# Neighbourhood attention of layer 0: ScalarE's copies and exponentials in turn, products with V ahead of the transposes, eight images written out

## The reference

```python
q = (x @ Wq + bq).reshape(B, nh, H, W, lr) * scale     # B 4, nh 8, H = W = 56, lr 4
k = (x @ Wk + bk).reshape(B, nh, H, W, lr)
v = (x @ Wv + bv).reshape(B, nh, H, W, hd)             # hd 32
k_win = k[:, :, idx_h][:, :, :, :, idx_w]              # the 7 x 7 keys around each token
v_win = v[:, :, idx_h][:, :, :, :, idx_w]
attn = jnp.einsum('bhijc,bhikjlc->bhijkl', q, k_win) + bias
attn = jax.nn.softmax(attn.reshape(B, nh, H, W, 49), axis=-1).reshape(B, nh, H, W, 7, 7)
out = jnp.einsum('bhijkl,bhikjld->bhijd', attn, v_win)
```

## Time and profile before

| what | value |
|---|---|
| median of 3 runs | 8468.63 us (8464.75 to 8475.0) |
| the profiled execution, its own time | 8475.56 us |
| its span, first to last instruction | 8473.8 us |
| `layer0_attend`, first score matmul to last store issued | 494.49 to 1606.54, 1112.05 us |
| TensorE busy share of the whole span | 86% |
| mean granted TensorE clock, whole span | 0.871 |
| mean granted TensorE clock, this stage | 0.59 |

### The profile page before, as it was taken

One profiled execution on the slowest core, in us unless ns is written; L12 is line 12 of the kernel. 1 busy time (PEld: TensorE's weight loads), 2 busy tenths in 40 slices (PEclk: granted clock), 3 DMA queues, 4 the chain that ended last, 5 costly groups with the idle time before them and its releaser, 6 DMA issues. The chain is left out here.

```text
span 8473.8 us, 153009 instructions
## 1 busy us (share of the span) xinstructions
PE 7312.5 (86%) x45616; PEld 4411.8 (52%) x45616; DVE 5407.8 (64%) x12877; ACT 4098.8 (48%) x9367; POOL 3701.9 (44%) x2395
## 2 busy tenths in 40 slices
PE   4457787898999999999999999999999888087877
PEld 3345565565545545455455455554553336076766
DVE  3357777666977767677677677776773017166666
ACT  0057777521025655556566566565656651033332
POOL 4010000111026666666666666566666663543432
PEclk8756555798579999999999999999999998598888
DMA  5432221487001120211210212112111016111110
GB/s 156 136 94 62 60 66 48 116 253 202 0 16 34 30 61 23 65 25 36 54 37 25 62 28 48 44 36 54 30 29 42 4 45 210 31 38 45 43 44 23
DMA packets 403203, 520.46 MB, mean 61 GB/s; under 512 B 64096, under 2 KB 355474, under 8 KB 399063
## 3 DMA queue, kind: packets, MB, share of 16 engines
q1 hardware_dynamic: 379687, 469.02, 20.6%
q0 software_dynamic: 22640, 40.75, 1.7%
HBM read 339.07 MB, written 200.10 MB: 64 GB/s over the span
## 5 line engine op out<-in xcount | busy, mean ns | idle before, releaser
L1253 DVE TENSOR_REDUCE a_tops<-a_ps 128x1 f32<-128x448 f32 (+1 forms) x5600 | 3070.8, 613 | 1085.6 <-PE a_ps L1155 1068.2
L1376 POOL TENSOR_TENSOR a_added<-a_P 128x896 f32<-128x896 f32 x1344 | 2800.3, 2104 | 2087.5 <-ACT a_P L1353 2087.5
L1353 ACT ACTIVATE a_P<-a_ps 128x448 f32<-128x448 f32 (+1 forms) x5600 | 2656.6, 547 | 2114.8 <-PE a_ps L1224 2083.0
L1224 PE MATMUL a_ps<-a_qp,a_kp 98*128 98x448 f32 (+1 forms) x5600 | 2155.6, 400 | 97.5 <-ACT a_P L1353 72.9
L1155 PE MATMUL a_ps<-a_hk,a_hq 96*128 96x448 f32 (+1 forms) x4900 | 1818.2, 381 | 1.9 <-DMA a_hq<-scratch_q 1.9
L1224 PEld LDWEIGHTS a_ps<-a_qp,a_kp 98*128 98x128 f32 (+1 forms) x5600 | 1029.7, 187 | 1289.5 <-ACT a_P L1353 736.3
L1175 PE MATMUL a_ps<-a_P,a_vt 128*32 128x448 f32 (+1 forms) x11200 | 1334.3, 548 | 0.0
L1155 PEld LDWEIGHTS a_ps<-a_hk,a_hq 96*128 96x128 f32 (+1 forms) x4900 | 916.6, 187 | 262.8 <-DVE a_tops L1253 170.9
L462 PE MATMUL n_ps<-n_idn,n_P 112*98 112x112 f32 x2688 | 523.6, 368 | 187.1 <-DVE n_P L519 168.0
L1191 PE MATMUL a_ps<-a_added,a_ones 128*32 128x448 f32 x5376 | 649.0, 555 | 0.0
L462 PEld LDWEIGHTS n_ps<-n_idn,n_P 112*98 112x98 f32 x2688 | 410.3, 181 | 288.2 <-DVE n_P L519 266.3
(11 more groups left out here) (193 smaller groups left out, 7674.9 us busy)
## 6 DMA issues: line engine op xcount, KB each, us to landing
a_qp<-scratch_q SPq DMA_DIRECT2D x168, 224.0 KB, 3.9
a_kp<-scratch_k SPq DMA_DIRECT2D x96, 320.0 KB, 5.5
a_hk<-scratch_k SPq DMA_DIRECT2D x84, 336.0 KB, 5.0
scratch_t<-o_ts SPq DMA_DIRECT2D x56, 448.0 KB, 5.6
scratch_vw<-scratch_v SPq DMA_DIRECT2D x56, 392.0 KB
n_vt<-scratch_vw SPq DMA_DIRECT2D x64, 343.0 KB
a_hq<-scratch_q SPq DMA_DIRECT2D x84, 200.0 KB, 3.2
e_w<-in_w SPq DMA_DIRECT2D x16, 1024.0 KB
```

Of the source, the lines that this page charges most:

```text
L1224: pe.matmul(PS[0:rows_of(t), i_s % 3, 0:GW], kp[0:98, hh, 128 * t:128 * t + rows_of(t)], qp[0:98, hh, GW * j:GW * j + GW], start=True, sto ...
L1253: dve.tensor_reduce(tops[0:rows_of(t), KT * hh + t, k:k + 1], PS[0:rows_of(t), bank, 0:GW], AX_X, ALU.max).then_inc(topped, 1)
L1353: act.activation(P[0:rows_of(t), (2 * n + pair) % (2 * RING), hh % 2, :], PS[0:rows_of(t), (4 * n + hh) % 3, 0:GW], ACT.Exp).then_inc(expe ...
L1376: pool.tensor_tensor(added2[:, a % 6, :, :], P[:, (2 * n + pair) % (2 * RING), :, :], P[:, (2 * n + 2 + pair) % (2 * RING), :, :], ALU.add ...
```

## The change

Four things change, all in `layer0_attend`. The computation and the number of matmuls, activations, VectorE instructions and DMAs stay as they are.

1. ScalarE takes the copies of the block before and the exponentials of this block in turn: C(n-1) head 0, E(n) head 0, C(n-1) head 1, E(n) head 1, and so on. The last four copies follow at the end of the stage.
2. TensorE does S(n), M(n-2), T(n-1), where it did S(n), T(n-1), M(n-2).
3. All eight images are written out on TensorE, ScalarE, VectorE, GpSimd and SyncE; the loops are gone, and waits compare with constants.
4. The increments of `steps` are gone with them.

```diff
             def body(it, first):
                 for n in range(NBLK):
                     scores(it, n)
+                    if n >= 2:
+                        mix(it, n - 2)
+                    elif not first:
+                        mix(it - 1, NBLK - 2 + n)
                     if n >= 1:
                         turn(it, n - 1)
                     elif not first:
                         turn(it - 1, NBLK - 1)
-                    if n >= 2:
-                        mix(it, n - 2)
-                    elif not first:
-                        mix(it - 1, NBLK - 2 + n)
 
             pe.wait_ge(consts, 16)
             pe.wait_ge(zeroed, 3)
-            body(0, True)
-            with pe.Fori(1, ITS) as it:
-                body(it, False)
+            for it in range(ITS):
+                body(it, it == 0)
+            mix(ITS - 1, NBLK - 2)
             turn(ITS - 1, NBLK - 1)
-            mix(ITS - 1, NBLK - 2)
             mix(ITS - 1, NBLK - 1)
...
-            def body(it):
+            def body(it, first):
                 for n in range(NBLK):
-                    exponentials(it, n)
-                    copy_turned(it, n)
-
-            body(0)
-            with act.Fori(1, ITS) as it:
-                body(it)
+                    for hh in range(4):
+                        if n >= 1:
+                            copy_turned(it, 4 * n - 4 + hh)
+                        elif not first:
+                            copy_turned(it - 1, U - 4 + hh)
+                        exponential(it, 4 * n + hh)
+
+            for it in range(ITS):
+                body(it, it == 0)
+            for hh in range(4):
+                copy_turned(ITS - 1, U - 4 + hh)
```

More of the change, by code:

```diff
@@ L325, in layer0_attend @@
         mixed, out_read, stored = sem("mixed"), sem("out_read"), sem("stored")
-        steps = sem("steps")
         def since(eng, semaphore, it, each, k):
-            if not isinstance(it, int) or it * each + k > 0:
+            if it * each + k > 0:
                 eng.wait_ge(semaphore, it * each + k)
@@ L369, in store, with body @@
                 sp.wait_ge(out_read, it * NBLK + 7 * (rb + 1))
-                sp.sem_inc(steps, 1)
                 since(sp, stored, it, 4 * 16, 16 * rb)
-                if not isinstance(it, int):
-                    sp.sem_inc(steps, 1)
                 at = slice(14 * W * rb, 14 * W * (rb + 1))
                 sp.dma_start(S["y0T"][b * 2 + g][:, at], yT[:, at]).then_inc(stored, 16)
-            def body(g, b, before, after, switch=False, switched=False):
-                it = g * B + b
+            def body(it):
+                g, b = divmod(it, B)
+                before = divmod(it - 1, B) if it > 0 else None
+                after = divmod(it + 1, B) if it < ITS - 1 else None
                 for rb in range(ROW_BLOCKS):
                     since(sp, mixed, it, NBLK, 7 * rb)
-                    if not isinstance(it, int):
-                        sp.sem_inc(steps, 1)
                     if rb < ROW_BLOCKS - 1:
@@ L392, in body @@
                         sp.wait_ge(placed, it * 8 + 8)
-                        if not isinstance(it, int):
-                            sp.sem_inc(steps, 1)
                         load_qk(*after)
-                    if switch and rb == 1:
+                    if it == B - 1 and rb == 1:
                         load_bias(1, 0)
-                    if switch and rb == 3:
+                    if it == B - 1 and rb == 3:
                         load_bias(1, 1)
-                    if switched and rb == 0:
+                    if it == B and rb == 0:
                         load_bias(1, 2)
@@ L409, in _ @@
             load_bias(0, 2)
[L410 to L417, removed]
+            for it in range(ITS):
+                body(it)
             store(1, B - 1, ITS - 1, ROW_BLOCKS - 1)
@@ L435, in _ @@
                 place(0, rb)
-            with pool.Fori(1, ITS) as it:
+            for it in range(1, ITS):
                 pool.wait_ge(loaded, (it + 1) * NLOAD)
@@ L439, in _ @@
                     pool.wait_ge(scored, it * U - U + 28 * (rb + 1))
-                    pool.sem_inc(steps, 1)
                     place(it, rb)
@@ L507, in maxima @@
                     dve.wait_ge(scored, it * U + m + 1)
-                    dve.sem_inc(steps, 1)
                     dve.tensor_tensor_reduce(out=sm[:, hh, :], in0=PS[0:TT, hh, 0:KEYS], in1=bias[:, hh, case, :],
@@ L542, in _ @@
             dve.memset(vt[0:14, :, :, 2, :], 0.0).then_inc(zeroed, 1)
[L543 to L548, removed]
+            for it in range(ITS):
+                body(it, it == 0, it % B == 0)
             read_out(ITS - 1, NBLK - 2)
@@ L553, in _, with exponential, copy_turned @@
         def _(act):
[L554 to L567, removed]
-            def body(it):
-                for n in range(NBLK):
-                    exponentials(it, n)
-                    copy_turned(it, n)
-            body(0)
-            with act.Fori(1, ITS) as it:
-                body(it)
+            def exponential(it, m):
+                act.wait_ge(maxed, it * U + m + 1)
+                since(act, turned, it, U, m - 7)
+                act.activation(P[:, m % 8, :], sm[:, m % 4, :], ACT.Exp, bias=mx[:, m % 8:m % 8 + 1], scale=-1.0,
+                               accum_out=rs[:, m % 8:m % 8 + 1]).then_inc(exped, 1)
+            def copy_turned(it, m):
+                if m % 4 == 0:
+                    since(act, mixed, it, NBLK, m // 4 - 1)
+                act.wait_ge(turned, it * U + m + 1)
+                act.activation(PTs[:, m % 8, :], PS[0:CHUNK, turn_bank(m), 0:3 * TT], ACT.Copy).then_inc(copied, 1)
+            def body(it, first):
+                for n in range(NBLK):
+                    for hh in range(4):
[4 more added lines that the diff above has]
+                        exponential(it, 4 * n + hh)
+            for it in range(ITS):
+                body(it, it == 0)
+            for hh in range(4):
+                copy_turned(ITS - 1, U - 4 + hh)
     nc.clear_and_free_semaphores(sems)
```

## The result

The changed kernel takes 8553.85 us (median of 4 runs, 8548.15 to 8559.53), the kernel before 8466.69 us beside it (8459.37 to 8475.0). The ratio is 1.0103 with a 95% interval of 1.0090 to 1.0115: 87 us slower. The forecast was 8565 us, 97 more than before.

A forecast was written before the change was run, and what follows sets the result against it. Order and waits, not one full engine, bound the stage. 221 x 5.34 = 1180, less 29 for fast blocks, plus 40 for GpSimd, is 1191 us against 1093.6, 97 more: 8565 us, range 8480 to 8645.

The forecast's parts named there:

- the chain: Last copy, M, T, first to last copy, through ScalarE and TensorE: closes and sets 5.34 us a block, against 4.64.
- last copy to first product: ScalarE's last copy of block n-2 to TensorE's M(n-2): 0.45 copy plus 0.12 semaphore, 0.57 us.
- product to transpose: On TensorE, M to the first T behind it: 1.28 us, taken from M followed by S; 0.97 from below.
- first copy to last copy: ScalarE's round with three exponentials between the copies: 3 x (0.35 + 0.52) = 2.61 us, where it was 1.62.
- block at clock 1.0: VectorE and ScalarE chain, last exponential through N and X to the next round: 4.50 us, against 4.01.
- blocks at clock 1.0: Of the stage's 221 blocks, 35 run at full clock, giving back 29 us; bounds 0 and 90 blocks.
- GpSimd's steps: Regrouping of q and k beside the stage: delayed scalings cost 40 us in all, between 20 and 60, against 52.
- turns of the loops: Writing out the six turns where the loops turn back saves 42 us; bounds 0 and 42.
- a clock that stays up: Rival: denser M, T, S on TensorE raises the clock in most blocks, 4.50 us each, 8410 us; chance 0.10.
- rounds that overlap freely: Rival: no chain closes through M and the copies; TensorE's own 4.27 us sets the block, 8370 us; chance 0.08.
- The one of no measurable change: Rival: a block about 0.4 us longer, just what the loops give back; chance 0.05.
- The rival at which the clock stays at 0.5: Rival: TensorE's clock stays at 0.5 throughout the stage, 127 us more, 8595 us; chance 0.22.

The follow-up runs named there:

- the fastest version: Changed kernel with TensorE back at S, T, M and VectorE's second pair of N moved behind the next block's first X: 8286.88 us, ratio 0.9807.

## Why the prediction was right

The direction, the chain and its place were as forecast. The sum was 22 us too high in the stage's distances, and the time 11 us. That it came so near is in part luck, since errors of 27 us and 13 us had opposite signs. By its own terms:

| term | forecast | measured |
|---|---|---|
| last copy to first product | 0.57 | 0.50 |
| product to transpose | 1.28 | 1.28 |
| first transpose to first copy | 0.89 | 0.89 |
| first copy to last copy | 2.61 | 2.55 |
| block at clock 0.5 | 5.34 | 5.22 |
| block at clock 1.0 | 4.50 | 4.44 |
| blocks at clock 1.0 | 35, giving back 29 us | 21, giving back 16 us |
| GpSimd's steps | 40 us | 35 us |
| turns of the loops | 42 us saved | no distance of 10 us left |
| 221 distances | 97 us more | 75.5 us more |

**The block.** 0.12 us too much a block is 27 us in 221. The way from a copy's end to TensorE was taken from a wait for VectorE, 0.12, and was 0.05. The rest is the pairs of a copy and an exponential. I took 0.35 and 0.52, 0.87 together; in the block above a copy is followed by its exponential after 0.35, 0.33 and 0.33, and that one by the next copy after 0.51 or 0.52, so a pair takes 0.85. The price of M followed by T, for which no row stood, was right to the hundredth, and the 0.7 at the upper clock is 0.71 in the timeline. The estimate from the Trainium skill (ScalarE: Activation LUTs, What ACT_TABLE_LOAD costs) was 0.79 for the pair; this case measures 0.85.

**The fast blocks.** The bound of 0 to 90 held. The value was too high, which took 13 us too much off the sum.

**GpSimd's steps.** I counted 32. The four of image 0 lie before the first R, so 28 fall into the stage's distances, and before the change each cost 1.9 us and not 1.6. The term of the sum was taken as a whole and does not change. How the 35 us come about was not seen: see R below.

**The loops.** The 42 us are shown twice: no long distance is left, and the written-out kernel alone has a stage 39.8 us shorter.

**The rivals.** Those of a clock that stays up and of rounds that overlap freely did not come. The latter's block of 4.27 needs two things that the change does not have: with M behind T alone the stage falls to 1036.2 us and blocks of 4.43, and only with VectorE's chain opened too are there blocks of 4.27. The one of no measurable change needed 0.97 from M to T, and it was 1.28. The rival at which the clock stays at 0.5 was nearest on the other side; the clock fell from 0.59 to 0.55, not to 0.50.

**What it did not see.** A second chain runs through R and is nearly as long. In the block above, the second exponential (707.03), reciprocal (707.68) and R (708.44) free bank 7 at about 708.83: R's 0.27 and the 0.12 of the earlier trace rows. The copy frees the product at 708.89. So the sum was right with only 0.06 us to spare, and only for undisturbed blocks: in 27 blocks beside GpSimd's steps R came last, and with R moved the time fell by 18 us, for the most part there. Where M is ahead of T but ScalarE works four and four, it is this chain that decides, and M's place costs 4.7%, 399 us.

**What each part is worth.** By the ratios to the kernel before, writing out alone gives 0.3%. Taking turns as well, with M behind T, gives another 0.4%. M ahead of T, with ScalarE in turn, then costs 1.7%. The change was two useful parts and one harmful one, and the harmful one is the order of two calls.

## What to carry to other kernels

When engines work through fixed lists, write down for each instruction that is moved what it waits for and what is queued behind it, and look for closed chains through two or three engines; add up each chain, the second longest too, since its length decides what the next edit does. A stage in which no engine is full, as in the earlier trace rows, asks for a chain to be opened, not for faster instructions. Test an edit made of several parts one part at a time: here the sum was 87 us slower, and two of its three parts were gains. When an experiment gives a few microseconds more than it should, look at which waits are gone: most of the 18 us of the moved R were a second chain at work in 27 blocks.

## What the runs showed that I had not expected

**The clock did not follow TensorE's busy share.** With TensorE back at S, T, M it was busy 946 of 1036 us at a mean clock of 0.54, as this row shows. In the fastest version it was busy 705 of 888 us, a smaller share, at 0.81.

```profile
502.52:1538.71 1036.19, 946.31 (x8841) 672.32 (x8838) 780.87 (x3316) 790.95 (x2654) 89.75 (x56) 0.54 0.23 58
```

Part of the busy time is itself longer at the lower clock, so these two shares alone do not tell cause from effect. But the fastest version has a long stretch in which TensorE had no idle time at all and the granted clock was 0.50 throughout:

```profile
1003.16:1032.69 29.53, 29.53 (x277) 21.76 (x277) 23.36 (x104) 23.76 (x82) 1.12 (x1) 0.50 0.19 49
```

In the same run TensorE was busy only 11.57 us of the 16.82 from 589.18 to 606.00, and the clock was 1.00. Such blocks of 3.59 us kept the upper clock until a step of GpSimd came. The Trainium skill (TensorE: Matmul & The Clock Gate, Why this matters for your kernels) advises to keep TensorE busy and without long idle gaps. The fastest version has no gap over 2.2 us in its distances, and the one at 0.54 none over 2.0, so that does not tell the two apart, and the stretch above goes against it: here the measurement decides. What lifts the clock in one and not in the other stays open.

**GpSimd's steps cost twice.** In the fastest version they cost 89 us by the medians and 113 by the ratios; its own ratio is the least certain one here (0.9781 to 0.9834). Its 221 distances fall from 887.8 to 798.5 us. The blocks at 4.27 go with them: 131 distances of 3.4 to 3.6 become 212 of 3.4 to 3.7. So part of the cost is the blocks made longer, and part is the blocks that ran at the lower clock after them. In the changed kernel the distances fall from 1169.1 to 1122.5.
